# One wider strip at the start of a graph-attention kernel, one narrower strip near its end

## The chip, the cores and the metric

The kernel runs on one core of a Trainium2 chip. The metric is the device time of one execution in microseconds (us), as a median over runs. The engines are TensorE (PE; its weight loads are PEld), VectorE (DVE), ScalarE (ACT), GpSimd (POOL) and SyncE (SP), which here issues nearly all transfers. Transfers are run by 16 DMA engines.

## The reference

```python
h = jnp.maximum(_layernorm(x, axis=-1), 0.0)          # x: 8192 x 128
# gnn(x=h, mask=adj, W, a_src, a_tgt), 4 heads:
proj = jnp.einsum('nf,hfo->hno', x, W)
s_src = jnp.einsum('hno,ho->hn', proj, a_src)
s_tgt = jnp.einsum('hno,ho->hn', proj, a_tgt)
scores = leaky_relu(s_src[:, :, None] + s_tgt[:, None, :], 0.2)
attn = jax.nn.softmax(mask[None] + scores, axis=1)    # adj: 8192 x 8192, values up to 1e9
vals = jnp.einsum('hij,hjo->hio', attn, proj) + x[None]
return elu(vals).mean(axis=0)                         # and the input x is added outside
```

The softmax runs down each column of adj. The entries of adj are so far apart that in each column one row takes all the weight. The kernel therefore looks for the row of the maximum of each column, adds the h of the column into that row of a table `sums`, and projects the sums. A check of this (`cert`, `hist`, `flag`) decides at run time whether a dense path has to be taken; it isn't taken for this input.

## The kernel before

**Strips.** adj (268 MB) is read once. It is cut into strips of columns, and WIDTHS gives the width of each in sets of 128 columns: 64 sets in all, in 23 strips, numbered Q = 0 to 22. `subs(g, i)` is the width of strip Q = 3g + i in sets, `sets_to` the number of sets before it. Each strip is loaded in G = 8 pieces r = 0 to 7 of 1024 rows each; a partition holds 8 rows of it. A set of a piece is 512 KB, so a piece of a 128, 256 or 384-wide strip is 512 KB, 1 MB or 1.5 MB, in contiguous rows of 512 B, 1 KB or 1.5 KB. The pieces go round a ring of 12 slots in SBUF. SP issues them in order (L373 to L383); a piece waits until the last chunk that read its slot has been turned (`turned_before`: for r >= 4 a chunk of the strip before, for r < 4 one of the strip before that). The pieces of the last strip need no slot of their own: they lie in the third set of the slots of the strip before (L310).

**Per strip.** DVE takes the elementwise maximum over the pieces (`piece_max`, L667 and L674; for wide strips the first set apart, L681) and finishes it with piece 7, set by set (`last_max`, L691). For each set PE turns the result (`turn_maxima`, L463), and DVE's `column_max` finds the column maximum (L699), writes the negative bias (L703) and marks the place (L704). Then each piece of the set is a "chunk": PE turns it into one of two PSUM banks (L495) and ACT takes its exp with the bias and sums it (L591), which says in which piece the maximum lies. There are 8 chunks per set. `order` says in which order the chunks of a strip come; with 2 sets it is (0,0), (1,0), (2,0), (0,1), (1,1), (2,1), (3,0), (3,1) and so on, as (piece, set). PE turns the maxima of the second set just before chunk 2, those of the third just before chunk 5.

**Rows found.** For the strip before, DVE finds the rows (`find_rows`, L711 to L720), PE turns them, DVE compares them (`find_same`, L728), PE sums equal ones (`sum_same`), ACT copies the sums (`copy_sum`, L612), DVE picks the target (`find_target`, L735 and L738), and POOL adds the rows into `sums` in DRAM by one indirect transfer per set (L436). IDX_AT, SUM_AT and COPY_AT give the chunks after which PE and ACT do their share; SOON gives earlier ones for one strip, in which DVE also does find_target earlier. NEXT_AT names strips in which PE turns the first maxima of the next strip within this one.

**Start.** SP issues strip 0, then x (4 transfers of 1 MB), then strip 1, then `clear_sums` (4.2 MB of zeros to `sums`, L369), then strip 2. Slot 11, the fourth piece of strip 1, overlaps the scratch of the layer norm, so SP waits for DVE first (L381, L382). DVE does `layer_norm` after the first strip's column maxima (L744 to L774); in it L767 is what SP waits for. ACT takes the square root after its chunks of strip 0 and then applies the norm (L604). The zeros for clear_sums are read from the tile `rows`, which copy_sum writes later.

**Tail.** When the last scattered add has landed, SP loads `sums` (L391 on), and PE, ACT, DVE and POOL project, apply elu and store.

Of the kernel before, what the change touches and what calls it, by code (L numbers as in the profile page):

```python
# [84 lines left out]
def peaked_path(nc, ctx, c, W, a_src, a_tgt, dense):  # L85
# [8 lines left out]
    G = 8  # L94
# [3 lines left out]
    NQ = 3  # L98
    WIDE = NQ * P
    BODY = 3  # L100
    WIDTHS = [1] + [NQ] * 20 + [2, 1]
    STRIPS = len(WIDTHS)
    LOOP_END = BODY * 6
    RING = 12
# [2 lines left out]
    FRONT = [(0, 0), (1, 0), (2, 0), (0, 1), (1, 1), (0, 2), (2, 1), (1, 2), (2, 2)]  # L107
    assert sum(WIDTHS) == NT and BODY * G % RING == 0
    assert all(n == NQ for n in WIDTHS[1:LOOP_END])
    F1 = F + 1  # L110
# [5 lines left out]
    def sem(name):  # L116
        return ctx.enter_context(nc.semaphore(name))
# [81 lines left out]
    s_cleared = sem("sums_cleared")  # L199
# [53 lines left out]
    def number(g, i):  # L253
        return g * BODY + i

    def former_of(g, i):
        return (g, i - 1) if i else (g - 1, BODY - 1)
# [4 lines left out]
    def known(g):  # L262
        return isinstance(g, int)

    def first_strip(g, i):
        return known(g) and number(g, i) == 0
# [4 lines left out]
    def subs(g, i):  # L271
        return WIDTHS[number(g, i)] if known(g) else NQ

# [4 lines left out]
    def sets_to(g, i):  # L278

        return sum(WIDTHS[:number(g, i)]) if known(g) else number(g, i) * NQ - (NQ - WIDTHS[0])  # L280

# [42 lines left out]
    def at(g, i, n):  # L324
        return sets_to(g, i) * G + n
# [14 lines left out]
    def added_before(engine, g, i):  # L340

        if not known(g) or number(g, i) > 1:
            engine.wait_ge(f_added, sets_to(*former_of(g, i)) * 16)

    def index_at(g, i):
        if known(g) and number(g, i) in SOON:
            return SOON[number(g, i)]
        nq = subs(g, i)
        return IDX_AT[nq], SUM_AT[nq], COPY_AT[nq]
# [1 line left out]
    IDX_AT = {1: 1, 2: 2, 3: 8}  # L351
    SUM_AT = {1: 2, 2: 4, 3: 13}
    COPY_AT = {1: 2, 2: 4, 3: 15}
    SOON = {STRIPS - 3: (6, 9, 10)}
    NEXT_AT = {STRIPS - 3: NQ * G - 1, STRIPS - 2: 13}
    CHECKS = 20
    WARM = 15
    OPENED = {2: 1, 0: 2, 1: 3}
# [1 line left out]
    with nc.Block() as block:  # L360
# [95 lines left out]
        def _(pe):  # L456
# [41 lines left out]
            def strip(g, i):  # L498
                nq, Q = subs(g, i), number(g, i)
                if not known(g) or Q not in [S + 1 for S in NEXT_AT]:  # L500
                    turn_maxima(g, i, 0)
                for n in range(nq * G):
# [3 lines left out]
                    if not first_strip(g, i):  # L506
                        if n == index_at(g, i)[0]:
                            turn_idx(*former_of(g, i))
                        if n == index_at(g, i)[1]:
                            sum_same(*former_of(g, i))  # L510
                    if known(g) and Q in NEXT_AT and n == NEXT_AT[Q]:
                        turn_maxima(*latter_of(g, i), 0)
# [68 lines left out]
        @block.scalar  # L581
        def _(act):
            def strip(g, i):
                nq, Q = subs(g, i), number(g, i)
                seen = set()
                for n, (r, q) in enumerate(order(nq)):
                    if q not in seen:
                        seen.add(q)
                        act.wait_ge(f_nb, sets_to(g, i) + q + 1)
                    act.wait_ge(f_turn, at(g, i, n) + 1)  # L590
                    act.activation(turned_ps[n % 2], turned_ps[n % 2], ACT.Exp, scale=KAPPA, bias=cert[:, i, q, G:G + 1],  # L591
                                   accum_out=cert[:, i, q, r:r + 1]).then_inc(f_exp, 1)
                    if not first_strip(g, i) and n == index_at(g, i)[2]:
                        copy_sum(*former_of(g, i))
                if first_strip(g, i):
                    layer_norm()

            def layer_norm():
                act.wait_ge(s_stat, 3)
                act.activation(half[:, :], var[:, :], ACT.Sqrt).then_inc(s_sqrt, 1)  # L600
                act.wait_ge(s_stat, 5)
                with act.Fori(0, NT) as t:
                    tile = h[:, bass.ds(t, 1), 0:F].rearrange("p t f -> p (t f)")
                    act.activation(tile, tile, ACT.Relu, scale=rstd[:, bass.ds(t, 1)],  # L604
                                   bias=nmr[:, bass.ds(t, 1)]).then_inc(f_h, 1)

            def copy_sum(g, i):

                nq = subs(g, i)
                act.wait_ge(f_sum, number(g, i) + 1)  # L610
                added_before(act, g, i)
                act.copy(rows[:, i, 0:nq, :], sum_ps[:, 0:nq, :]).then_inc(f_rows, 1)  # L612

            def stage_sums(k):
                act.wait_ge(t_turn, k + 1)
                if k >= 2:
                    act.wait_ge(t_p, (k - 1) * QUAD // 2)
                act.copy(stage[:, k % 2, :], agg_ps[k % 2]).then_inc(t_stage, 1)

            def fill(w):  # L620

                act.wait_ge(t_open, OPENED[w % 3])
                if w >= 3:
                    act.wait_ge(t_m, w - 2)
                act.activation(v_ps[w % 3], h_of(w), ACT.Relu, scale=PART, bias=part).then_inc(t_fa, 1)  # L625

            act.dma_start(a_row[0:1, 0], a_src.rearrange("(k h) o -> k h o", k=1)).then_inc(s_a, 16)
            act.dma_start(a_row[0:1, 1], a_tgt.rearrange("(k h) o -> k h o", k=1)).then_inc(s_a, 16)
            act.dma_start(w_sb[:, :, :], W.rearrange("h f o -> f h o")).then_inc(s_w, 16)
            act.sem_inc(f_exp, 2)  # L630
            act.wait_ge(s_const, 1)
            act.activation(h[:, :, F], first.to_broadcast([P, NT]), ACT.Exp, scale=-1.0).then_inc(s_weight, 1)
            strips_of(act, strip)
            copy_sum((STRIPS - 1) // BODY, (STRIPS - 1) % BODY)
            act.wait_ge(f_turn, NT * G)
            act.wait_ge(s_const, 2)
            act.activation(w_part, w_sb[:, :, :], ACT.Copy, scale=PART).then_inc(t_part, 1)
            fill(0)
            fill(1)
            stage_sums(0)  # L640
            stage_sums(1)
            for w in range(PAIRS):
                act.wait_ge(t_p, w + 1)
                if w >= 2:
                    act.wait_ge(t_m, w - 1)
                act.activation(e[w % 2], v_ps[w % 3], ACT.Exp, scale=1.0 / PART, bias=e_bias).then_inc(t_e, 1)  # L646
                k = w * 2 // QUAD + 2
                if (w + 2) % 3 != 2 and 3 <= w + 2 < PAIRS:
                    fill(w + 2)
                if w % 2 == 1 and k < NT // QUAD:  # L650
                    stage_sums(k)
            act.wait_ge(g_d, CHECKS)
            go = flag_of(act)
            with act.If(go > 0):
                act.wait_ge(d_begin, 1)
                dense["scalar"](act)

        @block.vector
        def _(dve):
# [117 lines left out]
            def strip(g, i):  # L777
                nq = subs(g, i)
                after, before = latter_of(g, i), former_of(g, i)
                last_max(g, i, 0)  # L780
                for q in range(nq):
                    if q + 1 < nq:
                        last_max(g, i, q + 1)
                    if q == nq - 1 and not first_strip(g, i) and not last_strip(g, i):
                        find_rows(*before)
                    if q == nq - 1 and not last_strip(g, i) and split(*after):
                        first_set_max(*after)
                    column_max(g, i, q)
                    if last_strip(g, i):
                        find_rows(*before)  # L790
                if first_strip(g, i):
                    layer_norm()
                soon = known(g) and number(g, i) in SOON
                if not last_strip(g, i) and nq == NQ or first_strip(g, i):
                    piece_max(*after, 1)
                    if not soon:
                        piece_max(*after, 2)
                if not first_strip(g, i):
                    find_same(*before)
                if not last_strip(g, i) and nq < NQ and not first_strip(g, i):  # L800
                    piece_max(*after, 1)
                    piece_max(*after, 2)
                if soon:
                    piece_max(*after, 2)
                if soon or nq == 2:
                    find_target(*before)
                if not last_strip(g, i):
                    piece_max(*after, 3)
                    piece_max(*after, 4)
                    piece_max(*after, 5)  # L810
                if not first_strip(g, i) and not soon and nq != 2:
                    find_target(*before)
                if not last_strip(g, i):
                    piece_max(*after, 6)
# [379 lines left out]
```

## Time and profile before

| | before |
|---|---|
| median of 3 runs | 894.34 us (894.29 to 894.96) |
| profiled execution: its own time | 894.86 us |
| its span | 893.1 us |
| PE, DVE, ACT, POOL busy | 691.0, 787.7, 696.2, 282.8 us |
| granted TensorE clock, mean | 0.97 |
| DMA moved | 294.43 MB, mean 330 GB/s |

The span is the time from the first to the last instruction in the profile; the execution's own time is a little longer. Busy time is the sum over an engine's instructions, and an engine that is busy for most of the span isn't for that reason the bound: what counts is which wait ends last in each stretch. All times inside the execution are counted from the start of the span.

### The profile page before, as it was taken

The page shows a single profiled execution, that of the slowest core. Times are in us where ns is not written, and L with a number is a line of the kernel's source. Part 1 is how long each engine was busy: PE and PEld are TensorE (multiplying, and loading weights), DVE is VectorE, ACT ScalarE, POOL GpSimd, SP SyncE. Part 2 cuts the span into 40 slices and gives each one's busy share as a digit, 9 for nine tenths or more (in the row PEclk, how much of TensorE's full clock was granted, in tenths as well). Part 3 has the DMA queues.
Part 4 walks back from the last instruction along what each step waited for, and adds up shares of the span by engine and source line. Part 5 has one row for each costly group of instructions (what it writes and reads, how often), then busy time and mean ns, then how long its engine had stood idle before and what let it go on. Part 6 is the DMA issues. An engine that isn't in the chain of part 4 may idle for free.

```text
span 893.1 us, 15102 instructions
## 1 busy us (share of the span) xinstructions
PE 691.0 (77%) x5026; PEld 560.2 (63%) x5026; DVE 787.7 (88%) x812; ACT 696.2 (78%) x1187; POOL 282.8 (32%) x161
## 2 busy tenths in 40 slices
PE   2405888888878878878888788788788788898995
PEld 1304777766766767767767667667667667764441
DVE  3975999999999999999999999999999998835887
ACT  0594878878868878879779778779788788886885
POOL 1000102232232333324323323422423324234886
PEclk9758899999999999999999999999999999999998
DMA  9999999999999999999999999999999999719713
GB/s 258 335 375 394 373 372 372 371 372 372 371 371 368 374 370 373 370 370 373 370 370 374 367 375 371 371 371 371 371 369 373 371 364 302 180 13 239 200 48 85
DMA packets 223849, 294.43 MB, mean 330 GB/s; under 512 B 4546, under 2 KB 218050, under 8 KB 223812
## 3 DMA queue, kind: packets, MB, share of 16 engines
q1 hardware_dynamic: 214064, 289.49, 94.4%
q0 software_dynamic: 9216, 4.20, 3.9%
q8 instruction: 21, 0.34, 0.2%
q10 hardware_dynamic: 532, 0.27, 0.1%
q14 instruction: 16, 0.13, 0.0%
HBM read 281.28 MB, written 12.65 MB: 329 GB/s over the span
## 4 chain that ended last, share of the span: by engine, by line
DMA 37%; PE 22%; DVE 21%; issue 10%; ACT 7%; SPq 2%; DVEq 0%; ACTq 0%; POOLq 0%
DMA arena<-in_adj 36%; PE ps L495 14%; DVE arena L699 7%; PE ps L463 6%; ACT ps L591 4%; DVE ps L704 4%; DVE arena L691 3%; SPq L383 2%; DVE arena L827 2%; ACT arena L646 1%; DVE arena L744 1%; DMA sums<-arena 1%; PE ps L534 1%; DVE arena L703 1%; PE ps L470 1%
## 5 line engine op out<-in xcount | busy, mean ns | idle before, releaser
L591 ACT ACTIVATE ps<-ps,arena 128x1024 f32<-128x1024 f32 x512 | 555.9, 1086 | 157.5 <-DVE arena L703 86.7
L495 PE MATMUL ps<-ident,arena 128*128 128x128 f32 x4096 | 541.2, 279 | 78.6 <-ACT ps L591 76.4
L495 PEld LDWEIGHTS ps<-ident,arena 128*128 128x128 f32 x4096 | 449.8, 142 | 156.6 <-ACT ps L591 153.0
L674 DVE TENSOR_TENSOR arena<-arena 128x3072 f32<-128x3072 f32 (+2 forms) x115 | 359.3, 3125 | 14.6 <-DMA arena<-in_adj 10.3
L436 POOL DMA_INDIRECT sums<-arena x64 | 179.4, 2803 | 508.4 <-DVE arena L738 210.8
L463 PE MATMUL ps<-ident,arena 128*128 128x128 f32 x512 | 69.8, 280 | 100.1 <-DVE arena L691 76.2
L463 PEld LDWEIGHTS ps<-ident,arena 128*128 128x128 f32 x512 | 57.4, 144 | 110.7 <-issue 68.4
L591 ACT ACTIVATION_READ_ACCUMULATOR ps<-ps,arena 128x1 f32 x512 | 100.3, 196 | 0.0
L699 DVE TENSOR_REDUCE arena<-ps 128x1 f32<-128x1024 f32 x64 | 78.2, 1222 | 15.5 <-PE ps L463 13.4
L691 DVE TENSOR_TENSOR arena<-arena 128x1024 f32<-128x1024 f32 x64 | 76.4, 1221 | 17.1 <-DMA arena<-in_adj 16.9
L704 DVE SCALAR_TENSOR_TENSOR ps<-ps,arena 128x1024 f32<-128x1024 f32 x64 | 82.1, 1282 | 0.0
L429 POOL COPY arena<-arena 128x27 f32 (+3 forms) x22 | 48.0, 2182 | 76.7 <-DMA sums<-arena 74.2
L534 PE MATMUL ps<-arena 128*128 128x512 f32 x128 | 60.7, 604 | 6.9 <-ACT ps L625 5.7
L667 DVE TENSOR_TENSOR arena<-arena 128x2048 f32<-128x2048 f32 (+2 forms) x23 | 51.5, 2241 | 8.2 <-DMA arena<-in_adj 8.1
L827 DVE SCALAR_TENSOR_TENSOR arena<-arena,ps 128x1024 f32<-128x1024 f32 x32 | 38.8, 1214 | 14.0 <-ACT arena L646 14.0
L449 POOL TENSOR_TENSOR arena<-arena 128x512 f32<-128x512 f32 x31 | 40.6, 1308 | 13.7 <-DVE arena L827 13.5
L534 PEld LDWEIGHTS ps<-arena 128*128 128x128 f32 x128 | 22.2, 189 | 35.8 <-issue 33.3
L646 ACT ACTIVATE arena<-ps,arena 128x1024 f32<-128x1024 f32 x32 | 35.6, 1111 | 8.4 <-PE ps L534 8.3
L681 DVE TENSOR_TENSOR arena<-arena 128x1024 f32<-128x1024 f32 x19 | 23.3, 1225 | 9.0 <-DMA arena<-in_adj 8.9
L604 ACT ACTIVATE arena<-arena,nmr,rstd x64 | 27.4, 494 | 3.5 <-DVE nmr L774 3.5
L625 ACT ACTIVATE ps<-arena 128x1024 f32<-128x1024 f32 x22 | 24.7, 1121 | 4.3 <-DVE arena L827 2.7
L453 POOL TENSOR_TENSOR arena<-arena 128x256 f32<-128x256 f32 x31 | 23.7, 764 | 5.2 <-DVE arena L847 3.4
(84 smaller groups left out, 225.5 us busy)
## 6 DMA issues: line engine op xcount, KB each, us to landing
arena<-in_adj SPq DMA_DIRECT2D x160, 1536.0 KB, 14.7
arena<-in_adj SPq DMA_DIRECT2D x16, 512.0 KB, 7.3
arena<-in_adj SPq DMA_DIRECT2D x8, 1024.0 KB, 10.5
sums<-arena SPq DMA_DIRECT2D x1, 4160.0 KB, 22.2
out<-arena SPq DMA_DIRECT2D x15, 256.0 KB, 2.6
arena<-sums SPq DMA_DIRECT2D x7, 512.0 KB, 8.0
sums<-arena POOLq DMA_INDIRECT x64, 8.5
arena<-sums SPq DMA_DIRECT2D x2, 256.0 KB, 3.1
```

The lines of the kernel that those rows point to most:

```text
L429: pool.tensor_copy(hist[:, bass.ds(sets_to(g, i), nq), :], cert[:, i, 0:nq, :]).then_inc(f_kept, 1)
L436: pool.indirect_dma_start(sums, bass.IndirectOffsetOnAxis(target[:, i, q:q + 1], 0), rows[:, i, q, 0:F], None, compute_op=ALU.add).then_in ...
L463: mm = pe.transpose(cells_ps[:, u * P:(u + 1) * P], acc_of(nq)[:, u, q * P:(q + 1) * P], ident[:, :])
L495: mm = pe.transpose(turned_ps[n % 2][:, m, :], piece(g, i, r)[:, m, q * P:(q + 1) * P], ident[:, :])
L534: mm = pe.matmul(v_ps[w % 3][:, i], stage[:, k % 2, at:at + P], w_part, start=False, stop=True, skip_group_check=True)
L591: act.activation(turned_ps[n % 2], turned_ps[n % 2], ACT.Exp, scale=KAPPA, bias=cert[:, i, q, G:G + 1], accum_out=cert[:, i, q, r:r + 1]). ...
L667: dve.tensor_tensor(acc_of(nq)[:, :, cols], piece(g, i, 0)[:, :, cols], piece(g, i, 1)[:, :, cols], ALU.max).then_inc(f_acc, 1)
L674: dve.tensor_tensor(acc_of(nq), acc_of(nq), piece(g, i, r), ALU.max).then_inc(f_acc, 1)
L691: dve.tensor_tensor(acc_of(nq)[:, :, cols], acc_of(nq)[:, :, cols], piece(g, i, G - 1)[:, :, cols], ALU.max).then_inc(f_max, 1)
L699: dve.tensor_reduce(cmx[:, i, q:q + 1], cells_ps[:, :], AX.X, ALU.max).then_inc(f_mx, 1)
L704: dve.scalar_tensor_tensor(cells_ps[:, :], cells_ps[:, :], cmx[:, i, q:q + 1], place, ALU.is_equal, ALU.mult, accum_out=in_range[:, i, q:q ...
L827: dve.scalar_tensor_tensor(m[:, w % 4], e[w % 2], PART, v_ps[w % 3], ALU.min, ALU.max).then_inc(t_m, 1)
```

## The change

WIDTHS is [2] + 19 x [3] + [2, 2, 1] in place of [1] + 20 x [3] + [2, 1]. There are 64 sets in 23 strips as before. Strip 0 is 256 wide instead of 128, strips 1 to 19 are 384 wide as before, strip 20 is 256 wide instead of 384, and strips 21 and 22 keep their widths. SOON moves from strip 20 to strip 19 (STRIPS - 4), and the entry of strip 20 in NEXT_AT goes. Since two sets of `rows` for strip 0 are now written over the zeros, ACT waits for the end of the clearing before that copy, and find_target isn't called in the first strip, which has no strip before it.

```diff
-    WIDTHS = [1] + [NQ] * 20 + [2, 1]
+    WIDTHS = [2] + [NQ] * 19 + [2, 2, 1]
...
-    SOON = {STRIPS - 3: (6, 9, 10)}
-    NEXT_AT = {STRIPS - 3: NQ * G - 1, STRIPS - 2: 13}
+    SOON = {STRIPS - 4: (6, 9, 10)}
+    NEXT_AT = {STRIPS - 2: 13}
...
                 act.wait_ge(f_sum, number(g, i) + 1)
+                if first_strip(g, i):
+                    act.wait_ge(s_cleared, 16)
                 added_before(act, g, i)
...
-                if soon or nq == 2:
+                if (soon or nq == 2) and not first_strip(g, i):
                     find_target(*before)
```

## Rows read from the trace of the kernel before

**Rows 1.** The page's slices: GB/s in 40 slices of the span.

```profile
GB/s 258 335 375 394 373 372 372 371 372 372 371 371 368 374 370 373 370 370 373 370 370 374 367 375 371 371 371 371 371 369 373 371 364 302 180 13 239 200 48 85
```

**Rows 2.** Windows: stretch, length, busy per engine, PE clock, DMA share, GB/s.

```profile
5.00:10.00 5.00, 2.63 (x4) 0.53 (x2) 1.43 (x2) 0.00 (x0) 0.00 (x0) 1.00 1.22 290
...
284.82:319.24 34.42, 28.37 (x225) 24.28 (x225) 32.62 (x30) 28.01 (x50) 11.07 (x5) 1.00 1.08 371
...
732.00:734.00 2.00, 0.56 (x5) 0.57 (x6) 1.84 (x2) 1.24 (x4) 0.83 (x1) 1.00 1.09 347
734.00:736.00 2.00, 2.00 (x20) 2.00 (x19) 1.84 (x4) 0.00 (x0) 0.00 (x0) 1.00 1.10 349
...
742.00:744.00 2.00, 2.00 (x20) 2.00 (x19) 1.27 (x2) 1.02 (x2) 0.00 (x0) 1.00 0.52 142
```

**Rows 3.** Timeline, start: the last step SP waits for, then strip 1's third and fourth pieces.

```profile
39.92 1.22 DVE L767 TENSOR_REDUCE wst<-arena 128x8 f32<-128x1024 f32 x1
...
46.27 3.36 DVE L674 TENSOR_TENSOR arena<-arena 128x3072 f32<-128x3072 f32 x1 [0.76 <-DMA arena<-in_adj]
50.49 3.36 DVE L674 TENSOR_TENSOR arena<-arena 128x3072 f32<-128x3072 f32 x1 [0.86 <-DMA arena<-in_adj]
```

**Rows 4.** Timeline, tail: first exps of strips 21, 22; first load of sums.

```profile
768.67 1.09 ACT L591 ACTIVATE ps<-ps,arena 128x1024 f32<-128x1024 f32 x1 [1.19 <-DVE arena L703]
...
789.88 1.09 ACT L591 ACTIVATE ps<-ps,arena 128x1024 f32<-128x1024 f32 x1
...
806.79 0.42 SPq L391 DMA_DIRECT2D arena<-sums  x1
```

**Rows 5.** Timeline: first L691 of strips 19 and 20, first exp of 20.

```profile
697.89 2.36 DVE L691 TENSOR_TENSOR arena<-arena 128x1024 f32<-128x1024 f32 x2 [0.87 <-DMA arena<-in_adj]
...
732.16 2.36 DVE L691 TENSOR_TENSOR arena<-arena 128x1024 f32<-128x1024 f32 x2 [0.77 <-DMA arena<-in_adj]
...
736.09 1.09 ACT L591 ACTIVATE ps<-ps,arena 128x1024 f32<-128x1024 f32 x1 [2.84 <-DVE arena L703]
```

**Rows 6.** DMA issues in 41.0 to 41.5: KB, us from issue to landing.

```profile
arena<-in_adj SPq DMA_DIRECT2D x1, 1536.0 KB, 9.3
```

**Rows 7.** Timeline, strip 2: the ends of the first two L704.

```profile
117.17 0.14 DVE L704 DVE_READ_ACCUMULATOR ps<-ps,arena 128x1 f32 x1
...
121.09 0.14 DVE L704 DVE_READ_ACCUMULATOR ps<-ps,arena 128x1 f32 x1
```

**Rows 8.** Strip 21's fifth and last piece: issue (timeline), then issue to landing.

```profile
743.56 0.54 SPq L383 DMA_DIRECT2D arena<-in_adj  x1
arena<-in_adj SPq DMA_DIRECT2D x1, 1024.0 KB, 5.5
...
751.33 0.54 SPq L383 DMA_DIRECT2D arena<-in_adj  x1
arena<-in_adj SPq DMA_DIRECT2D x1, 1024.0 KB, 8.6
```

**Rows 9.** Timeline, 42 to 87 us: ACT, DVE and POOL around strip 1.

```profile
42.39 27.35 ACT L604 ACTIVATE arena<-arena,nmr,rstd  x64 [3.46 <-DVE nmr L774]
67.28 2.36 DVE L691 TENSOR_TENSOR arena<-arena 128x1024 f32<-128x1024 f32 x2 [0.78 <-DMA arena<-in_adj]
72.32 1.28 ACT L591 ACT_TABLE_LOAD   x1 [2.58 <-PE ps L495]
77.51 0.19 POOL L429 COPY arena<-arena 128x9 f32<-128x9 f32 x1 [74.23 <-DMA sums<-arena]
86.70 1.23 DVE L681 TENSOR_TENSOR arena<-arena 128x1024 f32<-128x1024 f32 x1 [8.87 <-DMA arena<-in_adj]
```

**Rows 10.** Timeline, DVE: four maxima of strip 21; find_same of strip 20.

```profile
752.58 9.48 DVE L674 TENSOR_TENSOR arena<-arena 128x2048 f32<-128x2048 f32 x4
...
773.67 0.55 DVE L728 TENSOR_TENSOR arena<-ps,arena 128x384 f32<-128x384 f32 x1
```

**Rows 11.** Timeline, PE: chunks 3 and 4 of strip 21.

```profile
772.15 2.22 PE L495 MATMUL ps<-ident,arena 128*128 128x128 f32 x16
```

## The prediction

> **What bounds the kernel now.** I read the page's slices of 22.3 us first [rows 1]: GB/s stay near 371 in nearly all of them; only the first two and the last eight are clearly lower. Then I asked for windows [rows 2]. A 384-wide strip in the middle takes 34.42 us, of which DVE is busy 32.62 and ACT 28.01, and 371 GB/s move. Early on, DVE waits for each piece of strip 1, and they land 4.22 us apart (50.49 - 46.27) [rows 3]: 1.57 MB / 4.22 = 373 GB/s, the pure rate. So through the body the transfers set the pace, and a strip costs 8 x 4.22 = 33.8 us plus the small scattered adds. Two stretches differ. At the start the 128-wide strip moves at 290 GB/s. At the end transfers run dry (142 GB/s in 742 to 744) [rows 2] and are over by slice 35, at about 780 [rows 1], while the tail's first load is issued only at 806.79 [rows 4]. What lies between is the chain PE turn, ACT exp, 1.2 us a chunk. After 806.79 the change touches nothing, so I follow the time of that issue.
>
> **The frame.** I call "due" the start of the first L691 of a strip: all its pieces have landed and been reduced. Before, strip 19 is due at 697.89 and strip 20 at 732.16 [rows 5], 34.27 apart. After the change strip 19 is the last 384-wide strip, as strip 20 was, and strip 20 is 256 wide, as strip 21 was. SOON moves by one strip with them. Removing NEXT_AT's entry for that strip moves nothing: it put the next strip's turn after chunk 23, and turn_maxima at the head of the next strip is the same place in PE's order. So the work from strip 19 through the exps of the first 256-wide strip should repeat the old work from strip 20 through strip 21's. The new time is then: old end, plus what the start costs more, minus one body strip (34.27), plus one more 256-wide strip in the tail.
>
> **Start, transfers.** Strip 0 carries 8.39 MB where it carried 4.19. The old one at 290 GB/s took 14.5 us. For rows of 1 KB the trace has strip 21, at 347 and 349 GB/s while nothing was short [rows 2]: 8.39 / 0.348 = 24.1 us. That is +9.6. Bounds: 373 GB/s (rows of 1.5 KB) gives +8.0, 290 gives +14.4. I take 348, as it is the same shape. The Trainium skill, "DMA: Bandwidth & Descriptors", section Specifications, says that 512 B is enough for line rate. By it 1 KB rows would be no faster than 512 B ones, and the start would cost +14.4, not +9.6. The trace disagrees: 290, 348, 373 for 512 B, 1 KB, 1.5 KB.
>
> **Start, the gap.** The fourth piece of strip 1 goes into slot 11, where the layer norm has its scratch, so SP issues it only when DVE is through L767, at 39.92 + 1.22 = 41.15 [rows 3]. It landed 9.3 us later [rows 6], at 50.47, where DVE took it up (50.49), 4.22 behind the piece before: no gap. Now everything in front shifts by 9.6, and DVE has a second column_max before layer_norm. Its cost from a body strip, end of one L704 to the end of the next: 121.23 - 117.31 = 3.9 [rows 7]; the second L691 hides behind PE's turn. L767 ends at 41.15 + 9.6 + 3.9 = 54.65. On an empty queue 1 MB took 5.5 us from issue to landing [rows 8], of which 1.05 MB / 0.348 = 3.0 are data; so 1.5 MB takes 4.2 + 2.5 = 6.7, landing at 61.35. Without a gap it would land at 50.47 + 9.6 = 60.05. The gap is 1.3 us. Bounds: 0, if the queue is not yet dry, and 3.9, if landing takes 9.3 as before. Behind this DMA on SP stand all later pieces and the clearing of sums, so the gap is lost for good in a body set by transfers.
>
> **Start, what is hidden.** ACT has 16 chunks in place of 8 before its square root. They start 9.6 later than before plus nothing else, near 33.5, and take 16 x 1.2 us with two short waits, so they end near 53.5; the table load of 1.28 [rows 9] and the root put it at 55, where DVE, just through L767, wants it. The 27.35 us of L604 then end near 83.3 [rows 9]. The first exp stood 5.0 us behind strip 1's due time (72.32 - 67.28) [rows 9], so it is wanted at 67.28 + 10.9 + 5.0 = 83.2: ACT becomes just free. If it came 2 us late, the slots would still not be: strip 1's third set waits until 86.70 (then 97.6) for strip 2's landings [rows 9]. The new wait of ACT for s_cleared costs nothing: the clearing ended at 77.51 [rows 9], with the shift 88.4; the copy is chunk 15, after chunk 5 has waited for that third set. Leaving find_target out for the first strip removes nothing that existed, as strip 0 was not nq = 2. So strip 19 is due at 697.89 + 9.6 + 1.3 = 708.8, which is 23.4 before the old strip 20.
>
> **Tail, the added strip.** It counts from the first exp of one 256-wide strip to the first of the next. Three paths end there.
> ACT: 768.67 to 789.88, 21.2 us [rows 4]; the old next strip had only 512 KB pieces and was ready in time.
> DVE: from the first exp to the end of find_same (773.67 + 0.55), 5.55; six maxima of 256 columns, 2.37 each by four in 9.48, and find_target 0.6, together 14.8 [rows 10]; from the due time to the first exp, 736.09 - 732.16 = 3.93 [rows 5]. Sum 24.3.
> Transfers: the fifth piece waits for chunk 3 of the strip before, turned at 773.2, 4.5 after the first exp [rows 11]. It is issued on a dry queue: 5.5; three more pieces at 3.0 to 3.8 (the old ones landed from 743.56 + 5.5 = 749.06 to 751.33 + 8.6 = 759.93, three spacings in 10.9 [rows 8]) give 9.0 to 10.9; due time to first exp 3.9 again. Sum 22.9 to 24.8.
> The later path decides: 24.3 to 24.8, I take 24.6. So ACT stands idle for 3.4 us there. Bounds: 21.2, and 25.7 if every piece takes 3.9 us. The last strip's data (8 x 1.8 us behind that) lands about 10 us before DVE wants it, and the last three scattered adds hang on the same copy as before.
>
> **Sum.** 9.6 + 1.3 - 34.3 + 24.6 = +1.2 us. The profiled execution took 894.86 us (span 893.1), so 896.1; it lies 0.5 above the median 894.34, which gives 895.5. 0.2% is 1.8 us, about what a measurement can tell from no change.
>
> **Rivals.**
> (a) Tail at ACT's pace, faster. If the pieces of the added strip came as early as those of the old strip 22, it costs 21.2: sum -2.2, 892.1. With 1 KB rows at 373 and no gap it would be -5.1, 889.2. For it: both DVE and transfers are only 3 us over ACT. Against: two independent paths both come out over 24. It decides if both sink under 22.6. Chance 0.15.
> (b) The gap is larger. If slot 11 takes 9.3 us to land again, gap 3.9 and the sum is +3.8, 898.1. For it: the issue falls behind a DVE chain that I stretched from body rows. Against: 9.3 was with a full queue. Chance 0.11.
> (c) 1 KB rows are no faster than 512 B rows. Start +14.4; DVE's chain moves with it, the gap stays 1.3; sum +6.0, 900.3. For it: rows of one strip start 32 KB apart in either case, and strip 0 has 290. Against: strip 21's 348. Chance 0.06. This is what the rule in the section Specifications of the Trainium skill's page would do.
> (d) The added strip is held longer by transfers and adds: 25.7, sum +2.3, 896.6, on the same side of the bound as mine or just over. Chance 0.10.
> (e) Mine, +1.2; own range -0.8 to +3.2. Chance 0.58, of which some 0.17 lies above +1.8.
>
> **Range and chances.** 891.0 to 898.5 reaches into (a), holds (b), leaves (c) out. Slower by over 0.2%: 0.17 of (e), most of (b), all of (c), a few of (d), 0.34. Faster: (a), 0.15. Within: 0.51.
>
> **What would show it.** Strip 0 due near 28.4; L767 ending near 54.7; a slice of less than 373 GB/s just after 54; strip 1 due at 78.2, and every strip to 19 later by 10.9 than its number before (708.8). L703 of strip 21 some 24.5 after that of strip 20, with ACT idle 3.4 us before it and a dry queue about 4 us before strip 21's fifth piece. The tail's first load at 808.0. The forecast is wrong if strip 0's rate is not 348, if L767's chain is longer than counted, if the body is not set by transfers (then the shift of 10.9 would shrink strip by strip), or if the added strip costs under 22.6 or over 26.

## The result, and the profile after

Median of 7 runs 898.29 us (896.97 to 898.74), against 894.62 us (894.29 to 894.96, 7 runs) for the kernel before: ratio 1.0038, 95% interval 1.0028 to 1.0048. The change makes the kernel 3.7 us slower. The profiled execution took 898.66 us, span 896.8, 3.7 more than the one before. Three lines were added above, so L691, L699, L703 and L767 of before are L693, L701, L705 and L769 here.

The page's slices of the changed kernel, GB/s; the rows for comparison are [rows 1]:

```profile
GB/s 304 315 341 393 373 372 372 369 373 371 371 369 371 371 368 374 371 372 370 369 374 370 369 375 368 374 371 369 372 371 372 361 298 280 236 13 235 201 48 84
```

The first slice is higher than before (304 for 258: longer rows). The second and third are lower (315, 341 for 335, 375): x, which moves at 292 GB/s, comes later, and something is missing. The body is the same, and the last transfers of adj, in slices 32 to 34, come later than before. Timeline of the changed kernel (start, duration, engine, line):

```profile
28.93 2.36 DVE L693 TENSOR_TENSOR arena<-arena 128x1024 f32<-128x1024 f32 x2 [0.76 <-DMA arena<-in_adj]
...
53.95 1.22 DVE L769 TENSOR_REDUCE wst<-arena 128x8 f32<-128x1024 f32 x1
...
55.19 0.54 SPq L383 DMA_DIRECT2D arena<-in_adj  x1
...
78.53 2.36 DVE L693 TENSOR_TENSOR arena<-arena 128x1024 f32<-128x1024 f32 x2 [0.82 <-DMA arena<-in_adj]
...
709.94 2.36 DVE L693 TENSOR_TENSOR arena<-arena 128x1024 f32<-128x1024 f32 x2 [0.88 <-DMA arena<-in_adj]
...
746.45 1.09 ACT L591 ACTIVATE ps<-ps,arena 128x1024 f32<-128x1024 f32 x1 [1.19 <-DVE arena L705]
...
764.73 1.09 PE L495 MATMUL ps<-ident,arena 128*128 128x128 f32 x8 [0.20 <-ACT ps L591]
...
767.47 2.36 DVE L693 TENSOR_TENSOR arena<-arena 128x1024 f32<-128x1024 f32 x2 [0.96 <-DMA arena<-in_adj]
...
768.75 1.97 PE L463 MATMUL ps<-ident,arena 128*128 128x128 f32 x8 [2.93 <-DVE arena L693]
...
772.52 1.09 ACT L591 ACTIVATE ps<-ps,arena 128x1024 f32<-128x1024 f32 x1 [5.46 <-PE ps L495]
...
810.47 0.41 SPq L391 DMA_DIRECT2D arena<-sums  x1
```

The four lines L693 are the due times of strips 0, 1, 19 and 21. Strip 0 is due 10.1 later than before (18.83), strip 1 11.25 later [rows 9], strip 19 12.05 later [rows 5]. From the due time of strip 19 to the first exp of strip 20 it takes 36.51 us (746.45 - 709.94), exactly what the old kernel took from the due time of strip 20 to the first exp of strip 21 (768.67 - 732.16) [rows 4, 5]: the frame of the prediction holds. The added strip, first exp to first exp, takes 772.52 - 746.45 = 26.07. From the first exp of strip 21 to the first load of sums it is 37.95, against 38.12. So the 3.68 us between 806.79 and 810.47 add up as 12.05 - 34.27 + 26.07 - 0.17.

Windows of the changed kernel around the two suspicious places (stretch, length, busy PE, PEld, DVE, ACT, POOL, clock, DMA share, GB/s):

```profile
50.00:54.00 4.00, 2.33 (x18) 1.72 (x16) 3.86 (x18) 3.90 (x9) 0.00 (x0) 1.00 1.07 373
54.00:55.00 1.00, 0.00 (x0) 0.00 (x0) 1.00 (x1) 1.00 (x1) 0.00 (x0) 1.00 0.75 263
55.00:56.00 1.00, 0.00 (x0) 0.00 (x0) 0.93 (x4) 0.33 (x2) 0.00 (x0) 1.00 0.13 46
56.00:57.00 1.00, 0.00 (x0) 0.00 (x0) 1.00 (x2) 0.48 (x2) 0.00 (x0) 1.00 0.40 94
57.00:58.00 1.00, 0.00 (x0) 0.00 (x0) 1.00 (x1) 1.00 (x4) 0.00 (x0) 0.79 1.00 310
...
766.00:768.00 2.00, 0.00 (x0) 0.00 (x0) 1.04 (x2) 1.06 (x2) 1.44 (x1) 0.89 1.19 312
768.00:770.00 2.00, 1.25 (x6) 1.25 (x7) 1.83 (x2) 0.00 (x0) 0.10 (x1) 0.50 1.08 281
```

The gap at slot 11 is there. What did not flow in 54 to 58, against 373 GB/s, is 110 + 327 + 279 + 63 = 779 GB/s over one microsecond each; divided by 373, that is 2.1 us of transfer. And in the tail TensorE's granted clock fell to 0.5, its lower level of 1.2 GHz, while it did nothing from 765.82 to 768.75, and the turn of strip 21's maxima took 1.97 us where the prediction had it at the 1.1 of the body.

### The profile page after: what moved, and what is told of

Read it like the earlier page. It is cut to its first block, busy times and chain, and to the rows that moved or that the text cites. A ratio compares the mean times of both kernels' runs of the same rounds, so it can differ in the third digit from the quotient of the medians.

```text
span 896.8 us, 15146 instructions
## 1 busy us (share of the span) xinstructions
PE 692.8 (77%) x5026; PEld 561.8 (63%) x5026; DVE 787.4 (88%) x811; ACT 695.8 (78%) x1187; POOL 280.2 (31%) x161
## 4 chain that ended last, share of the span: by engine, by line
DMA 37%; PE 22%; DVE 19%; issue 12%; ACT 7%; SPq 3%; DVEq 0%; ACTq 0%; POOLq 0%
DMA arena<-in_adj 36%; PE ps L495 14%; DVE arena L701 7%; PE ps L463 6%; ACT ps L591 4%; DVE arena L693 3%; SPq L383 3%; DVE ps L706 2%; DVE arena L829 2%; ACT arena L648 1%; DVE arena L746 1%; PE ps L534 1%; DMA sums<-arena 1%; DVE arena L705 1%; PE ps L470 1%
## 5 line engine op out<-in xcount | busy, mean ns | idle before, releaser
L701 DVE TENSOR_REDUCE arena<-ps 128x1 f32<-128x1024 f32 x64 | 78.2, 1222 | 17.3 <-PE ps L463 15.3
L693 DVE TENSOR_TENSOR arena<-arena 128x1024 f32<-128x1024 f32 x64 | 76.3, 1221 | 18.2 <-DMA arena<-in_adj 18.0
L429 POOL COPY arena<-arena 128x27 f32 (+2 forms) x22 | 46.3, 2107 | 89.8 <-DMA sums<-arena 86.2
L669 DVE TENSOR_TENSOR arena<-arena 128x2048 f32<-128x2048 f32 (+2 forms) x23 | 52.6, 2286 | 10.9 <-DMA arena<-in_adj 10.9
L449 POOL TENSOR_TENSOR arena<-arena 128x512 f32<-128x512 f32 x31 | 40.6, 1309 | 13.7 <-DVE arena L829 13.6
L604 ACT ACTIVATE arena<-arena,nmr,rstd x64 | 27.4, 494 | 1.2 <-DVE nmr L776 1.2
```

Of the source, the lines that this page charges most:

```text
L429: pool.tensor_copy(hist[:, bass.ds(sets_to(g, i), nq), :], cert[:, i, 0:nq, :]).then_inc(f_kept, 1)
L669: dve.tensor_tensor(acc_of(nq)[:, :, cols], piece(g, i, 0)[:, :, cols], piece(g, i, 1)[:, :, cols], ALU.max).then_inc(f_acc, 1)
L693: dve.tensor_tensor(acc_of(nq)[:, :, cols], acc_of(nq)[:, :, cols], piece(g, i, G - 1)[:, :, cols], ALU.max).then_inc(f_max, 1)
L701: dve.tensor_reduce(cmx[:, i, q:q + 1], cells_ps[:, :], AX.X, ALU.max).then_inc(f_mx, 1)
```

## The experiments

All stand on the changed kernel where nothing else is said. The columns "strip 0", "strip 1" and "strip 10" give how much later (us) the strip is due than in the kernel before, the last column the time from the first exp of strip 20 to that of strip 21. These four are of one profiled execution each; the medians are of all runs. E1 to E4 ran on one chip and E5 to E10 on another; each ratio is taken against the kernel before on the same chip.

| kernel | median us (runs) | ratio to before, 95% | strip 0 | strip 1 | strip 10 | first exp 20 to 21 |
|---|---|---|---|---|---|---|
| changed | 898.29 (7) | 1.0038, 1.0028 to 1.0048 | 10.10 | 11.25 | 12.09 | 26.07 |
| E10, changed again | 898.12 (5) | 1.0036, 1.0022 to 1.0050 | 10.01 | 11.39 | 11.87 | 24.93 |
| E1, product early | 895.60 (11) | 1.0012, 1.0003 to 1.0021 | 10.03 | 10.20 | 10.05 | 24.82 |
| E2, PE kept busy | 897.57 (7) | 1.0027, 1.0016 to 1.0039 | 10.33 | 11.78 | 12.70 | 24.84 |
| E3, rows of 512 B | 902.99 (4) | 1.0092, 1.0076 to 1.0107 | 14.51 | 16.19 | 16.80 | 25.96 |
| E4, 256 in the body | 901.69 (5) | 1.0078, 1.0064 to 1.0091 | 9.96 | 11.79 | 11.97 | other |
| E5, product later | 900.32 (5) | 1.0062, 1.0049 to 1.0076 | 10.03 | 15.20 | 15.55 | 25.79 |
| E6, tail 1, 1 | 902.44 (5) | 1.0083, 1.0070 to 1.0097 | 10.14 | 12.04 | 12.13 | other |
| E7, before, product early | 894.77 (11) | 1.0000, 0.9991 to 1.0009 | 0.03 | 0.27 | -0.32 | none |
| E8, E1 and E2 | 895.46 (11) | 1.0006, 0.9996 to 1.0015 | 10.20 | 10.28 | 10.20 | 24.78 |
| E9, E8 and order | 894.78 (11) | 0.9998, 0.9989 to 1.0007 | 10.06 | 10.25 | 10.44 | 24.38 |

**E1: the gap closed.** The product of W and the attention vectors needs nothing of x. It is taken out of the layer norm and goes where DVE waits for its first pieces (only the place where it goes is shown).

```diff
+            dve.wait_ge(s_w, 16)
+            dve.wait_ge(s_spread, 1)
+            for k in range(2):
+                ins = dve.tensor_tensor(a_w[:, k], w_sb[:, :, :], a_ps[:, k], ALU.mult)
...
+            dve.tensor_reduce(wst[...], a_w, AX.X, ALU.add).then_inc(s_set, 1)
```

> The changed kernel, with the product of W and the attention vectors and its reduction (DVE, 2.5 us) moved from the layer norm to ahead of strip 0's maxima, where DVE waits for its first pieces anyway. In the changed kernel SP could issue slot 11 only at 55.19, and DMA stood at 263, 46, 94 and 310 GB/s in the four microseconds 54 to 58. Theory A (that gap, 1.15 us, is one of the terms, and every microsecond of it is carried to the end by a body set by transfers): SP issues near 52, no microsecond under 370 GB/s, strip 1 due 1.1 to 1.3 earlier, time 1.1 to 1.3 us under the changed kernel's 898.3, so near 897.1, ratio to the kernel before near 1.003. Rival B (the body has slack and absorbs a small gap): strip 1 earlier, the end unmoved, 898.3.

Measured: 895.60, 2.7 under the changed kernel. Windows and timeline of E1:

```profile
54.00:55.00 1.00, 0.00 (x0) 0.00 (x0) 0.00 (x0) 1.00 (x1) 0.00 (x0) 1.00 1.08 372
55.00:56.00 1.00, 0.00 (x0) 0.00 (x0) 0.66 (x2) 0.27 (x2) 0.00 (x0) 0.50 1.07 376
56.00:57.00 1.00, 0.00 (x0) 0.00 (x0) 1.00 (x2) 0.55 (x2) 0.00 (x0) 0.50 1.06 373
```

```profile
51.95 9.32 SPq L383 DMA_DIRECT2D arena<-in_adj  x4
...
762.60 1.09 PE L495 MATMUL ps<-ident,arena 128*128 128x128 f32 x8 [0.20 <-ACT ps L591]
766.49 1.09 PE L463 MATMUL ps<-ident,arena 128*128 128x128 f32 x8 [2.79 <-DVE arena L693]
```

SP issues slot 11 at 51.95, no microsecond is short, and from strip 2 to strip 18 the strips are due 2 us earlier than in the changed kernel (strip 10: 10.05 against 12.09). Nothing is absorbed: rival B falls. The gap was worth 2.0 and not the 1.15 that I had read off strip 1 when I wrote this expectation. The other profiles agree: strip 10 is due 11.87 to 12.70 later than before in the five with the changed kernel's start as it is (the changed kernel, E2, E4, E6, E10), and 10.05 to 10.44 in the three with the product moved (E1, E8, E9). The remaining 0.7 of the difference of the medians is not traced. The profiled execution, at 894.58 the shortest of the eleven, is 4.1 under that of the changed kernel, and 1.25 of it is a second term: PE stood idle 2.79 us before strip 21's turn, and its clock did not fall (the turn took 1.09).

**E2: PE kept busy.** 20 transposes of the identity behind strip 20's last chunk; their result is not used.

```diff
+                if known(g) and Q == STRIPS - 2:
+                    for _ in range(20):
+                        pe.transpose(idx_ps[:, 0, :], ident[:, :], ident[:, :])
```

> The changed kernel, with 20 transposes of the identity into an unused PSUM bank after strip 20's last chunk, where PE stood idle from 765.8 to 768.75 and its granted clock fell to 0.5 until about 774. Theory A (the cold clock is 1.1 us of the added strip's cost: turn 1.97 us in place of 1.06, first chunk late): clock 1.00 throughout, from strip 21's due time to its first exp 3.9 us in place of 5.05, time about 1.1 us lower, near 897.2. Rival B (what follows is set by another path, the turn's lateness is hidden): turn faster, time unmoved at 898.3. The 20 transposes take 2.7 us at full clock; if they end after DVE's maxima, up to 0.3 us is lost.

Measured: 897.57, 0.7 under the changed kernel, intervals overlapping. Timeline and windows of E2:

```profile
766.14 2.35 PE L502 MATMUL ps<-ident 128*128 128x128 f32 x20
769.13 1.09 PE L463 MATMUL ps<-ident,arena 128*128 128x128 f32 x8 [0.64 <-DVE arena L696]
```

```profile
768.00:770.00 2.00, 1.36 (x13) 1.13 (x12) 2.00 (x2) 0.00 (x0) 0.63 (x1) 1.00 1.06 279
```

The clock stays at 1.00, the turn takes 1.09, and the added strip 24.84 in place of 26.07. The median gains less than 1.2, and the gain is not clear of noise. E10 gives one reason: the clock falls in some executions of the changed kernel and not in others. Another is that in E2's profile the body is 0.6 later (strip 10: 12.70 for 12.09), for which I have no cause. The Trainium skill, "TensorE: Matmul & The Clock Gate", Part 1, says that the clock has a full and a half level and goes back to the half one after idling; these traces agree for the two levels. They also show that about the same idle time can go either way: the clock fell after 2.93 us (changed), 2.83 (E3) and 2.85 (E5), and stayed after 2.92 (E10) and 2.79 (E1).

**E3: the same bytes in rows of 512 B.** Each piece of strip 0 comes in two transfers; its readers wait for both (not shown).

```diff
+                    if first_strip(g, i):
+                        sp.dma_start(piece(g, i, r)[:, :, 0:P], adj_r[r, :, :, 0:P]).then_inc(f_half[r], 16)
+                        sp.dma_start(piece(g, i, r)[:, :, P:2 * P], adj_r[r, :, :, P:2 * P]).then_inc(f_in[slot(i, r)], 16)
+                        continue
```

> The changed kernel, with each piece of strip 0 loaded by two transfers of 128 columns (rows of 512 B) in place of one of 256 (rows of 1 KB): same bytes. Theory A (the rate hangs on the row's length: 290 GB/s for 512 B, 348 for 1 KB): strip 0 due 4.8 us later, near 33.7, and the end later by as much, near 903.1, since the layer norm's chain moves with it. Rival C (rows of 512 B already run at line rate, and the 290 of the old strip 0 is a matter of the start or of the 32 KB pitch): strip 0 due near 29, time 898.3.

Measured: 902.99, 4.7 over the changed kernel, for 4.8 expected. Windows, first of the changed kernel in strip 0, then of E3, then of the changed kernel while x is loaded:

```profile
10.00:15.00 5.00, 0.00 (x0) 0.00 (x0) 3.47 (x2) 0.00 (x0) 0.00 (x0) 1.00 1.09 349
```

```profile
10.00:15.00 5.00, 0.00 (x0) 0.00 (x0) 2.29 (x1) 0.00 (x0) 0.00 (x0) 1.00 1.22 290
```

```profile
32.00:42.00 10.00, 8.96 (x67) 7.81 (x66) 8.34 (x25) 6.99 (x13) 0.00 (x0) 1.00 1.04 292
```

Rows of 512 B in place of 1 KB make 349 into 290 GB/s. E3 also halves the size of a transfer, from 1 MB to 512 KB, but that is not the cause: x comes in transfers of 1 MB, each from one contiguous block and again in rows of 512 B, and moves at 292. That also leaves out the 32 KB between the rows of a strip. Strip 0 is due 4.4 later than in the changed kernel, strip 10 4.7.

**E4: the second 256-wide strip in the body.** `split` is false for the strip behind it, whose accumulator would otherwise be written too early.

```diff
-    WIDTHS = [2] + [NQ] * 19 + [2, 2, 1]
+    WIDTHS = [2] + [NQ] * 18 + [2, NQ, 2, 1]
-    SOON = {STRIPS - 4: (6, 9, 10)}
-    NEXT_AT = {STRIPS - 2: 13}
+    SOON = {STRIPS - 3: (6, 9, 10)}
+    NEXT_AT = {STRIPS - 3: NQ * G - 1, STRIPS - 2: 13}
```

> Widths 2, 18 x 3, 2, 3, 2, 1: the same strips as the changed kernel, but the second 256-wide strip stands before the last 384-wide one, so that the tail is that of the kernel before (SOON and NEXT_AT as there). Theory A (the added strip costs 26.1 us in the tail, where PE, ACT, DVE and the slots stand in a chain, and 24.1 us of transfer plus 0.4 of adds where transfers set the pace, unless its own slots starve them): 1.5 us under the changed kernel, near 896.8, and up to 2 us worse than that if the queue runs dry at its fifth piece as it did in the tail. Rival D (a 256-wide strip costs the same wherever it stands): 898.3.

Measured: 901.69, 3.4 over the changed kernel instead of 1.5 under it: a miss. Timeline and windows of E4 at strip 19, the 256-wide one:

```profile
675.49 2.36 DVE L693 TENSOR_TENSOR arena<-arena 128x1024 f32<-128x1024 f32 x2 [0.79 <-DMA arena<-in_adj]
...
686.90 0.54 SPq L383 DMA_DIRECT2D arena<-in_adj  x1
...
704.18 2.36 DVE L693 TENSOR_TENSOR arena<-arena 128x1024 f32<-128x1024 f32 x2
```

```profile
684.00:686.00 2.00, 1.97 (x18) 1.97 (x19) 1.12 (x6) 1.91 (x3) 0.00 (x0) 1.00 0.89 246
686.00:688.00 2.00, 1.74 (x16) 1.51 (x14) 1.93 (x3) 0.89 (x3) 0.00 (x0) 1.00 0.16 32
688.00:690.00 2.00, 1.26 (x10) 1.03 (x10) 2.00 (x3) 1.91 (x5) 1.39 (x1) 1.00 0.79 262
```

The fifth piece is issued 11.4 us after the due time of the strip before, when that strip's third set has been turned for the first piece. Behind a 384-wide strip four pieces of 1 MB, 12 us at 348 GB/s, are queued by then, partly moved already, and the queue runs dry; in a pure body there are four of 1.5 MB, 16.9 us. The strip takes 28.7 us in place of the 24.5 of its bytes and adds. With it the sum against the kernel before is 12.0 - 34.3 + 28.7 = +6.4, where the profiled execution has +6.75, so at most 0.3 is left for the missing split. The changed kernel has the same hole in its tail, before strip 21's fifth piece:

```profile
748.00:750.00 2.00, 2.00 (x20) 2.00 (x19) 1.37 (x3) 0.95 (x3) 1.47 (x2) 1.00 0.63 182
750.00:752.00 2.00, 1.91 (x17) 1.58 (x15) 1.97 (x6) 1.94 (x3) 0.00 (x0) 1.00 0.26 33
```

There most of it is hidden, since ACT and DVE have 21 to 24 us of work for the strip; in the body it is paid. So the narrow strip is better off at the end, and rival D falls too.

**E5: the gap widened.** Four products that serve nothing, before the one SP waits for.

```diff
+                for n in range(4):
+                    dve.tensor_tensor(a_w[:, 0], w_sb[:, :, :], a_ps[:, 0], ALU.mult).then_inc(s_more, 1)
+                    dve.wait_ge(s_more, n + 1)
```

> The changed kernel, with four more products of 128x512 (about 0.65 us each with their waits, 2.6 us) on DVE in the layer norm ahead of L769, which SP waits for. They serve nothing. Theory A (slot 11's issue is already behind the queue's end, so each further microsecond is lost in full): SP issues near 57.8, gap and strip 1's due time later by 2.6, end later by 2.6, near 900.9. Rival B (slack in the body): less than half of it at the end.

Measured: the four products took 2.9 (0.72 each with its wait), and DVE came to them 0.5 later than in the changed kernel (53.16 for 52.64), because its second column_max had waited 1.82 for PE in place of 1.25. So SP issued at 58.60, 3.4 later than in the changed kernel, and strip 10 was due 15.55 - 12.09 = 3.5 later: one for one in this execution. Row of E5's timeline:

```profile
58.60 3.65 SPq L384 DMA_DIRECT2D arena<-in_adj  x3
```

The median rose by only 2.0 to 2.2, less than the 2.6 expected but more than rival B's half of it. E5's profiled execution, 902.46, was the longest of its five; what the others got back I did not find.

**E6: a shorter tail.**

```diff
-    WIDTHS = [2] + [NQ] * 19 + [2, 2, 1]
+    WIDTHS = [2] + [NQ] * 20 + [1, 1]
-    SOON = {STRIPS - 4: (6, 9, 10)}
-    NEXT_AT = {STRIPS - 2: 13}
+    SOON = {STRIPS - 3: (6, 9, 10)}
+    NEXT_AT = {STRIPS - 3: NQ * G - 1}
```

> Widths 2, 20 x 3, 1, 1 (SOON at strip 20, NEXT_AT at strip 20 only): start as in the changed kernel, the tail after the last 384-wide strip has 16 chunks in place of 24. Theory A (start costs 12.05 over the kernel before; everything through strip 20 as before, then a 128-wide strip in place of a 256-wide one takes about 10.9 in place of 21.2 from first exp to first exp): 12.05 - 10.3 = +1.8 on the kernel before, near 896.4, and worse by 1 to 3 us if DVE or the three scattered adds of strip 20 are late for the shorter strips. Rival E (the tail is bound by the transfers of the last strips, not by PE and ACT): +4 or more.

Measured: 902.44, 7.7 over the kernel before where 1.8 was expected; a miss. The size is that of rival E, but its mechanism is not what the trace shows, for the transfers stood idle from 785 to 790. Timeline of E6:

```profile
770.80 1.23 DVE L693 TENSOR_TENSOR arena<-arena 128x1024 f32<-128x1024 f32 x1
...
780.42 0.19 DVE L713 SCALAR_TENSOR_TENSOR arena<-arena 128x24 f32<-128x24 f32 x1 [8.40 <-ACT ps L591]
...
782.65 1.09 ACT L591 ACTIVATE ps<-ps,arena 128x1024 f32<-128x1024 f32 x1 [2.25 <-DVE arena L705]
...
796.39 1.09 ACT L591 ACTIVATE ps<-ps,arena 128x1024 f32<-128x1024 f32 x1 [3.83 <-DVE arena L705]
```

In a strip of one set, find_rows (L713) stands ahead of the only column_max on DVE's queue, and it waits for all exps of the strip before. So the bias comes late, ACT stands idle, and the next strip's maxima are late in turn: 13.7 us from first exp to first exp for the 10.9 expected, and 1.1 more on the strip before it. Of the 5 us that the profiled execution is over the expected sum, these are 3.9; 0.7 more lies in the due time of strip 20, and 0.45 behind the last strip's first exp.

**E7: E1's move on the kernel before.**

> The kernel before, with the same move of the product as in the first experiment. There slot 11 was issued at 41.17 with the queue still full (landing 9.3 us later, 4.22 behind the piece before). Theory A: nothing to gain, 894.6 within 0.5. Rival F (DVE's layer norm is on the path there too, since DVE works without a break after it): 2.4 us less.

Measured: 894.77 against 894.76 on the same chip, ratio 1.0000 (0.9991 to 1.0009). There the queue was still full at slot 11 [rows 6], so there was no gap to close. Rival F falls.

**E8 to E10: both edits, the order of chunks, and the changed kernel again.** E8 is E1 and E2 in one. E9 adds, for strip 20 alone:

```diff
+    def order_of(g, i):
+        if known(g) and number(g, i) == STRIPS - 3:
+            return [(0, 0), (1, 0), (0, 1), (1, 1), (2, 0), (2, 1)] + [(r, q) for r in range(LEAD, G) for q in range(2)]
+        return order(subs(g, i))
```

> The changed kernel with both edits of the first two experiments: the product ahead of strip 0's maxima, and 20 transposes that keep TensorE's clock up before strip 21. The first took 2.7 us off the median (and its profiled execution happened to keep the clock at 1.00 without help), the second 0.7. Theory A (the gap and the cold clock are separate terms): strip 19 due 9.9 to 10.2 over the kernel before, first exp of strip 20 to that of strip 21 24.8, time 0.7 to 1.2 under the first experiment's 895.6, near 894.7, level with the kernel before, and a narrower spread of its runs. Rival (they are the same loss counted twice): 895.6, spread as before.

> As e8, and in strip 20 alone the chunks go (0,0), (1,0), (0,1), (1,1), (2,0), (2,1) in place of (0,0), (1,0), (2,0), (0,1), (1,1), (2,1), so that the slot of strip 20's first piece comes free one chunk earlier, and with it the issue of strip 21's fifth piece on a queue that has run dry. In the changed kernel DVE waited 0.96 us for these pieces before strip 21's first L693. Theory A (strip 21's due time hangs on that issue, with DVE's own path 0.9 behind): fifth piece issued 1.1 earlier, strip 21 due 0.5 to 0.9 earlier, end as much earlier, near 894.1. Rival G (DVE's own work sets the due time): issue earlier, DVE's wait gone, end unmoved or 0.3 later.

> The changed kernel itself, on the same chip as these two, so that their medians can be compared with it directly. Its ratio to the kernel before was 1.0038 (1.0028 to 1.0048). All theories: 898.3 within 0.5. Its profile shows what varies from one execution to the next: whether the clock of TensorE falls at strip 21, and the due times of strips 1 and 2.

Measured on one chip: E8 895.46, E9 894.78, the changed kernel 898.12, the kernel before 894.95. E8 is not the sum of the two gains. It is 0.5 over the kernel before on its chip, where E1 was 0.9 over it on the other, and the intervals overlap. Its 11 runs spread over 1.2 us (894.90 to 896.08) where E1's spread over 2.5 (894.58 to 897.08). That the steady clock narrows the spread is not shown by this: the kernel before, 17 times on E1's chip, spread over 2.5 as well. In E9 strip 21's fifth piece was issued at 748.03, against 749.10 in E8. ACT now waits longer for strip 20's second bias (the first row below), and the added strip takes 24.38 for 24.78, so theory A gives 0.4 where 0.5 to 0.9 was hoped. From the first exp of strip 20 to strip 21's due time E9 gains 0.7 (20.15 for 20.84), and DVE no longer waits for a transfer there. Of this 0.3 is lost again, because the 20 transposes end at 766.64, after the turn of strip 21's maxima could have begun. Timeline of E9:

```profile
748.61 1.09 ACT L599 ACTIVATE ps<-ps,arena 128x1024 f32<-128x1024 f32 x1 [1.62 <-DVE arena L713]
...
769.07 1.09 ACT L599 ACTIVATE ps<-ps,arena 128x1024 f32<-128x1024 f32 x1 [3.37 <-DVE arena L713]
```

E9 can't be told from the kernel before (0.9989 to 1.0007). No version beat both kernels. The same stretch in E10, the changed kernel once more, window and turn:

```profile
768.00:770.00 2.00, 1.36 (x12) 1.37 (x13) 1.95 (x3) 0.00 (x0) 0.02 (x1) 1.00 1.10 281
```

```profile
768.64 1.09 PE L463 MATMUL ps<-ident,arena 128*128 128x128 f32 x8 [2.92 <-DVE arena L693]
```

Here the clock did not fall, after an idle time of 2.92 us against 2.93. This execution took 897.04 where the other profiled one took 898.66, and 1.14 of that is in the added strip.

## Why the prediction was right or wrong

It said +1.2 us, with half of the chance within 0.2% and 0.34 on slower; +3.7 was measured, or 0.38%. The direction and the frame were right. In the profiled execution three terms were larger than predicted: the start by 0.5, the gap by 0.7 and the added strip by 1.5, of which 1.2 is the clock.

That 898.29 lies inside 891.0 to 898.5, by 0.2, is luck. My own case (e) reached only to +3.2. The range went further to hold rival (b), whose 898.1 is near the measured time for another reason: slot 11's piece landed 6.5 us after its issue and not 9.3, and the gap was 2.0 and not 3.9. What (b) puts into the gap beyond that came from the start and the added strip. The sign "over 26" of the added strip was met too, by 26.07 in the first profile, though not by the 24.93 of E10. Rival (a), under 22.6, was met by no profile.

**Right.** *The frame.* The shifts of the due times stay constant from strip 4 to 19 within 0.25 us, so the body is set by transfers; the profiles of E1 and E5 show that what the start gains or loses arrives at the end of the body one for one. The stretch from the last 384-wide strip to the next first exp is the same to 0.01 us. *Strip 0 at 348 GB/s.* 349 measured, and E3 shows that the row's length does it: rival (c) falls. By the rule of the Trainium skill, "DMA: Bandwidth & Descriptors", section Specifications, strip 0 in rows of 1 KB should have taken as long as in rows of 512 B. The 4.4 us between their due times say otherwise. Strip 0 came at +10.1 for +9.6: the pieces came 3.02 apart as computed, and about 0.4 more passed before the first two were there. *The hidden parts.* ACT's root was ready at 55.35, DVE wanted it at 55.37; L604 ended at 83.87, 0.3 after strip 1's exps would have begun by the old distance of 5.04 from the due time, and this moved no due time: in E1, where it ended at 83.80, 1.3 after that point, the body is still only 10.05 later, as strip 0 is; the new wait for the clearing was not seen. *The added strip, apart from the clock.* 24.6 predicted, 24.8 to 24.9 in all four profiles where the clock held and the order was unchanged (E1, E2, E8, E10). DVE waited 0.96 for the last piece of strip 21 after the four maxima, so of the two paths the transfers' was the later, as predicted, though by 0.96 and not by the half microsecond it was given.

**The gap, mis-sized: 1.3 predicted, 2.0 measured.** The step "1.5 MB takes 4.2 + 2.5 = 6.7, landing at 61.35; without a gap at 60.05" had the right times: SP issued at 55.19, the piece landed 6.5 later, at 61.7. But the difference of two landings is not the time lost. A piece has landed when the last of the 16 DMA engines is through with its part, and the trace marks each engine's end. In E1, on a full queue, the engines end slot 11's piece from 59.00 to 60.68; in the changed kernel, on the emptied queue, from 61.38 to 61.69. So the last engine is 1.0 late and the first 2.4, and the landing shows only the last. The windows count 2.1 us without flow; strip 1 was due only 1.15 more late than strip 0, strip 10 2.0 more. E1 confirms 2.0.

**The clock, left out: 1.2 in some executions.** The prediction put this term at nothing. In "due time to first exp, 3.9 again" I took PE's turn from a place where PE had not stood idle. My own sum had ACT, and so PE, idle for 3.4 us ahead of it, and still used the full-clock duration; a row for the low level was at hand in the start of the kernel before, where PE had been idle too: strip 1's turn took 1.97 us at a granted clock of 0.50. In the first profiled execution due time to first exp took 5.05, in E10 3.93.

**Sum.** 10.1 + 2.0 - 34.3 + 26.07 - 0.17 = 3.7 with the clock down, about 2.5 with it up. The tail's own difference from 22.8 (two sets at the body's 11.4) is the larger part of the loss: one 256-wide strip among PE, ACT, DVE and freed slots costs 2 to 3.3 us more there than two sets cost in the body. The start costs 12.05 for 11.42; with the gap closed it is 10.0, cheaper than a set in the body.

**Open.** The kernels with the changed kernel's start have strip 1 due at 78.53 to 79.32 without a difference in the code there, and slot 11's time of issue does not explain it (55.06 with 79.07 in E4, 55.19 with 78.53 in the changed kernel). How often the clock falls is not known, for only profiles show it. E5's timed runs lie nearer to the changed kernel than its profile does. Whether one of the two paths could bring the added strip under 24.3 was tried only by E9.

## What to carry to other kernels

When a transfer waits for an engine's result, compare the time of its issue with the end of the queued transfers: here an issue at 55.19, with the piece ahead landing at 56.4, was too late, and one at 51.95 was in time. Count what is lost in GB/s windows, not in the first landing behind it. Work ahead of the wait that does not need the late data can be moved into an earlier idle stretch. A change from large to small pieces in a ring can open a hole at the change itself: the pieces queued must last until the first slot of the new strip comes free. When your own sum says that TensorE stands idle before a step on the path, price the step at its low clock as well.

## What the runs showed of the hardware that I had not expected

After nearly the same idle time of TensorE, the granted clock fell to 0.5 in three profiles (2.83, 2.85 and 2.93 us idle) and stayed at 1.00 in two (2.79 and 2.92). The 2.93 and the 2.92 are of one and the same program, and its added strip took 26.07 us with the fall and 24.93 without. And, without anything short on the queue, contiguous rows of 512 B, 1 KB and 1.5 KB moved at 290, 349 and 373 GB/s on the same queue.
